# Three products of constants per slot, added to open sums in 14 of 104 slots of each batch but the last

## The chip, the cores and the metric

The kernel runs on one core of a Trainium2 chip. The metric is the device time of that core in microseconds (us); before the change the median of three runs is 1739.21 us (1738.99 to 1742.22). Engines by their short names: PE is TensorE (PEld its weight loads), DVE VectorE, ACT ScalarE, POOL GpSimd, SP SyncE. PEclk is the clock that TensorE was granted, as a share of 2.4 GHz: 1.00 is 2.4 GHz, 0.50 is 1.2 GHz, and a value between them is a mean over a stretch that has both.

## The reference

```
h = concat(x[:, 0:744], x[:, 3:747], x[:, 6:750]) @ W.T + b      # 8 x 744 x 256
q, k, v = heads(layernorm(h));  att = softmax(causal(q k^T / 4)) # 16 heads of 16
h = h + (att v) @ Wp.T + bp
x2 = layernorm(h);  logits = x2 @ wr + br;  top 2 of 4 experts, gates = softmax(top 2)
out = h + sum over the 2 chosen of gate * (y_e - c_e + c_sum),  y_e = gelu(x2 @ w1_e + b1_e) @ w2_e + b2_e
```

Here x is 8 x 750 x 256 in fp32, c_e is the expert's output for a zero input, and c_sum the sum of the four.

## The kernel before

Attention goes batch by batch (8 batches). A batch's 744 positions are 6 tiles of 124, and its 16 heads are 4 groups of 4. For every group the scores are formed twice. First in rows (`mx`, tile mxb, line 1409), from which DVE takes each row's maximum (lines 1040 and 1043, result mxp); the maxima are turned on PE (line 1415), made negative and split on DVE (negp) and sent by SP's queue into qst, the stack of queries. Then in columns (`st`, tile stb, line 1428), from which ACT makes the exponentials (prob, line 857) and POOL masks the diagonal (line 709). Products with the values (`pv`, line 1453) add up in two banks called pvb; the 17th of their output rows per head is the sum of weights. mxb and stb have two buffers each, so PE can be two steps ahead of DVE and of ACT.

The order is written out by hand. `body_events` makes the list of a batch: 104 slots, 26 for each group. Slot s begins with `st` s, then come the `mx` steps due there, then what `put(s, ...)` sets beside it. Every engine runs through the same list and does its own part, in order. So one batch's attention lies beside the previous batch's end (`proj`, the output projection and second norm, line 1389 on PE and 1074 on DVE; `scale2`, `gate`, `count`, `scatter`, the routing to experts) and beside the next batch's front (`tok`, the input layer; `xn`, its norm, DVE line 1013; `turn`, its transposes, PE line 1363; `qk`, its queries and keys, line 1341 with xnT and qkvw, from which ACT, DVE and POOL make `parts` that SP stores to qk_s and loads again as stacks qst and kst).

Points that matter here:

- `turn` 2 and 3 stand in slots 35 and 36 and wait for all six `xn`, the last of which DVE makes in slot 34.
- `st` 26 g waits for the negated maxima of group g (negm_loaded): slots 0, 26, 52 and 78.
- `mx` of the next batch's first group begins in slot 67 and waits for its stack (stack_loaded).
- `pv` of group 0 stands in slots 12, 20, 24, 28, 28 and 30, that of group 1 in 38, 46, 50, 54, 54 and 56. A sum in the second bank is open from a group's first `pv` to its last.
- `earlier` is a 124 x 124 bf16 constant, 1 above the diagonal and 0 elsewhere, so its column 0 is zero; `every` is all ones. Both serve `count` (lines 1397, 1398).

After the eighth batch the experts run: 34 tiles of 384 tokens, `l1` (line 1505) and `l2` (line 1521).

Of the kernel before, what the change touches and what calls it, by code (L numbers as in the profile page):

```python
# [16 lines left out]
TT = T // NT  # L17
HALF = T // 2
NH, DH = 16, 16
# [41 lines left out]
LEAD = 12  # L61
PV_LAG = 4
PB = 3


def part_at(n, t):
# [4 lines left out]
def later(value):  # L71

    return not isinstance(value, int) or value > 0


def mx_events(first, last):

    for u in range(first, last):
        yield "mx", u
        g, k = divmod(u, NMX)  # L80
        if g and k in (1, 3, 4):
            yield {1: "mx_row", 3: "mx_turn", 4: "mx_neg"}[k], g - 1
# [23 lines left out]
def pv_events(g):  # L106

    for o in range(NT):
        yield NST * g + PV_AFTER[o] + PV_LAG, ("pv", (g, o))
    yield NST * (g + 1) + PV_LAG + 1, ("pv_copy", g)  # L110


def body_events(first, last):


    beside = {}

    def put(s, *event):
        beside.setdefault(s, []).append(event)

    for g in range(-1 if not first else 0, NG):
        for s, event in pv_events(g):
            if 0 <= s < NG * NST:
                put(s, *event)
    for i in range(NT):
        put(5 + i, "v", i)
        if not last:
            put(11 + 2 * i, "tok", i)
        if not first:
            put(23 + 2 * i, "proj", i)  # L130
    if not first:
        put(6, "fold", -1)
        put(10, "recip", -1)
        put(11, "spread_out", -1)
        put(14, "spread_in", -1)
        put(1, "scale", -2)
        put(20, "scale", -1)
        put(4, "late_stack", 2)
        put(19, "late_stack", NG - 1)
        put(36, "norm2", 0)  # L140
        for i, s in enumerate((39, 40, 42, 43, 45, 46)):
            put(s, "scale2", i)
        put(42, "h2_store", 0)
        for p, s in enumerate((48, 49, 51, 52)):
            put(s, "gate", p)
        put(54, "count", 0)
        put(55, "place", 0)
        put(56, "place", 1)
        for i, s in enumerate((58, 61, 64, 67, 71, 74, 78, 81, 84, 88, 91, 95)):
            put(57 + 2 * i if last else s, "scatter", i)  # L150
    for g, s in ((0, 45), (1, 60), (2, 86)):
        put(s, "fold", g)
    put(73, "recip", 0)
    put(75, "spread_out", 0)
    put(79, "spread_in", 0)
    for n, (load, split, store) in enumerate(((2, 10, 13), (19, 26, 29), (47, 57, 62), (67, 76, 98))):
        if last:
            load, split, store = ((2, 8, 11), (14, 19, 21), (24, 29, 31), (34, 39, 41))[n]
        put(load, "wload", n)
        put(split, "wsplit", n)  # L160
        put(store, "wstore", n)
    if not first:
        put(7, "res_load", -1)
    if last:
        put(64, "res_load", 0)
    if not last:
        for p in range(2 * KC):
            put(2 + 2 * p, "x", p)
        put(22, "norm", 0)
        for i in range(NT):  # L170
            put(24 + 2 * i, "xn", i)
        for n, s in enumerate((30, 32, 35, 36)):
            put(s, "turn", n)
        for p, s in enumerate((35, 36, 37)):
            put(s, "bias", p)
        put(53, "h1_store", 0)
        for n in range(4):
            put(38 + 3 * n, "qk", n)
            put(59 + 3 * n, "qk", n + 4)
        put(51, "load_stack", 0)  # L180
        put(72, "load_stack", 1)
        put(35, "x_load", 1)
    else:
        for s, kind in ((68, "mx_row"), (70, "mx_turn"), (72, "mx_neg")):
            put(s, kind, NG - 1)
        for m, s in enumerate(W2_SLOT):
            put(s, "w2_load", m)
        put(30, "early_consts", 0)
        put(58, "early_table", 0)
        put(50, "small_load", 0)  # L190
        put(74, "early_load", 0)
        put(86, "early_load", 1)
    mx_at = NMX + LEAD
    mx_end = NG * NMX if last else NG * NMX + NMX + LEAD
    for s in range(NG * NST):
        want = min(NMX + LEAD + (s + 1) * NMX // NST, mx_end)
        g, k = divmod(s, NST)
        yield "st", s
        yield from mx_events(mx_at, want)
        mx_at = max(mx_at, want)  # L200
        for o in range(NT):
            if PV_AFTER[o] == k + 1:
                yield "mask", (g, o)
        yield from beside.get(s, ())
# [124 lines left out]
def layer(nc, xT, tokWT, tokW, tokb, wkT, wqT, wvT, wpT, wp, bp, bcols, wr, br, wall, h1_s, qk_s, r_s, out, ws, xs, b1T, b2, base):  # L329
    with ExitStack() as es:  # L330
        memory = ExitStack()

        def sb(name, shape, dt=fp32):
            return memory.enter_context(nc.sbuf_tensor(name, shape, dt))

        def ps(name, shape):
            return memory.enter_context(nc.psum_tensor(name, shape, fp32))
# [14 lines left out]
        h1 = sb("h1", [TT, NT, DA])  # L352
        parts = sb("parts", [128, PB, NPART, HALF], bf16)
        rest = sb("rest", [128, 2, HALF])
# [39 lines left out]
        earlier = sb("earlier", [TT, TT], bf16)  # L394
        every = sb("every", [TT, TT], bf16)
# [25 lines left out]
        pvb = ps("pvb", [128, 2, 512])  # L421
# [48 lines left out]
        def sem(name):  # L470
            return es.enter_context(nc.semaphore(name))
# [9 lines left out]
        qk_mid, qk_low = sem("qk_mid"), sem("qk_low")  # L481
        parts_stored = [sem(f"parts_stored{i}") for i in range(PB)]
        stack_loaded = [sem(f"stack_loaded{g}") for g in range(NG)]
# [45 lines left out]
        def _(sp):  # L529
# [12 lines left out]
            def emit(events, b, a):  # L542
                for kind, n in events:
                    if kind == "qk":
# [3 lines left out]
                                     .rearrange("t r h c -> (r h) t c"),  # L548
                                     parts[:, (a * 8 + n) % PB, :, :]).then_inc(parts_stored[(a * 8 + n) % PB], 16)
                    if kind in ("load_stack", "late_stack"):  # L550
                        to = a if kind == "load_stack" else b

                        for i in range(PB):
                            sp.wait_ge(parts_stored[i], 16 * ((to * 8 + n // 2 * 4 + 3 - i) // PB + 1))
                        if later(to):
# [40 lines left out]
                    if kind == "w2_load":  # L596

                        sp.wait_ge(v_full, NB * NT)
                        sp.wait_ge(h1_stored, NB * 16)
                        for i in range(PB):  # L600
                            sp.wait_ge(parts_stored[i], 16 * ((NB * 8 - 1 - i) // PB + 1))
# [705 lines left out]
        def _(pe):  # L1307
            pe.wait_ge(raw_loaded, 32)
            for c in range(3 * KC):
                for k in range(KC):  # L1310
                    done = nc.tensor.matmul(pab[:, NE * c:NE * c + NE], tok_raw[:, k, 128 * c:128 * c + 128], wr_sb[:, k, :],
                                            start=(k == 0), stop=(k == KC - 1))
# [3 lines left out]
            for c in range(KC):  # L1316
                for k in range(KC):
                    nc.tensor.matmul(pabs[1][:, 24 + NE * c:24 + NE * c + NE], wp_rows[:, k, 128 * c:128 * c + 128], wr_sb[:, k, :],
                                     start=(k == 0), stop=(k == KC - 1))
            for n in range(3):  # L1320
                for k in range(KC):
                    side = ones[:, :] if n == 2 else bcol[:, k, n:n + 1].broadcast_to([128, TT])
                    done = nc.tensor.matmul(pabs[1][0:TT, 40 + NE * n:40 + NE * n + NE], side, wr_sb[:, k, :],
                                            start=(k == 0), stop=(k == KC - 1))
# [5 lines left out]
            def take_bank(pab, by, value):  # L1330

                k = pabs.index(pab)
                if bank_by[k] is not None:
                    pe.wait_ge(*bank_by[k])
                bank_by[k] = (by, value)
# [8 lines left out]
            def emit(events, b, a):  # L1344
                for kind, n in events:
# [3 lines left out]
                    if kind == "tok":  # L1349
                        if n == 0:  # L1350
                            pe.wait_ge(x_split, a * KC + KC)
                        take_bank(pab, tok_evac, a * NT + n + 1)
                        split_product(pab[0:TT, 0:DA],
                                      [[xp[p][:, c, TT * n + o:TT * n + o + TT] for o in SHIFTS for c in range(KC)] for p in range(2)],
                                      [[tokw[p][:, c, :] for c in range(3 * KC)] for p in range(2)]).then_inc(tok_full, 1)
                    if kind == "turn":
                        c, half = n % 2, n // 2
                        if a == 0 and n == 0:
                            pe.wait_ge(consts, 5)
                        pe.wait_ge(xn_ready, a * NT + 3 * half + 3)  # L1360
                        take_bank(pab, turn_evac, a * 4 + n + 1)
                        for i in range(3):
                            done = nc.tensor.transpose(pab[:, TT * i:TT * i + TT], xn[:, 3 * half + i, 128 * c:128 * c + 128],
                                                       ident[0:TT, 0:TT])
                        done.then_inc(turn_full, 1)
# [18 lines left out]
                    if kind == "proj":  # L1384
# [3 lines left out]
                        for c in range(KC):  # L1388
                            done = nc.tensor.matmul(pab[0:TT, 0:DA], yT[:, c, TT * n:TT * n + TT], projw[:, c, :],
                                                    start=(c == 0), stop=(c == KC - 1))  # L1390
# [8 lines left out]
                    if kind == "mx":  # L1399
                        g, k = divmod(n, NMX)  # L1400
# [15 lines left out]
                    if kind == "st":  # L1416
                        g, k = divmod(n, NST)
# [8 lines left out]
                        for j, h, q0, w in ST[k]:  # L1426
                            out = stb[n % STB][0:TT, at:at + w]
                            done = nc.tensor.matmul(out, kst[g][:, h, TT * j:TT * j + TT], qst[g][:, h, q0:q0 + w],  # L1428
                                                    start=True, stop=True)
                            at += w  # L1430
                        done.then_inc(st_full, 1)
                    if kind == "pv":
# [11 lines left out]
                        for s in range(2):  # L1444
# [3 lines left out]
                            for h in range(HG):  # L1448
                                if j in prob:
                                    p = prob[j][0:TT, h, q0 - TT * j:q1 - TT * j]  # L1450
                                else:
# [3 lines left out]
                                                        stop=(j == (2 if s == 0 else 4)))  # L1455
# [117 lines left out]
```

## Time and profile before

| | before |
|---|---|
| median of 3 runs | 1739.21 us |
| profiled execution | 1728.33 us |
| its span, first to last instruction | 1726.6 us |
| mean granted clock | 0.937 |
| PE busy | 1523.0 us (88%) |
| DVE busy | 1101.6 us (64%) |
| POOL busy | 836.9 us (48%) |
| ACT busy | 707.3 us (41%) |

The shares are means over stages that differ: from 98.5 us to 1054.8 us the eight batches run, from about 1180 us on the experts alone. Slots have no record of their own; where one begins is read from its `st` product (line 1428), since the shapes of these come in a fixed order and all 1024 are in the trace. In batch 1, slot 24 begins on PE at 240.5 us, slot 28 at 245.4, slot 34 at 252.7, slot 36 at 256.2, slot 41 at 262.8, slot 52 at 279.5 and slot 60 at 289.7.

### The profile page before, as it was taken

The page shows a single profiled execution, that of the slowest core. Times are in us where ns is not written, and L with a number is a line of the kernel's source. Part 1 is how long each engine was busy: PE and PEld are TensorE (multiplying, and loading weights), DVE is VectorE, ACT ScalarE, POOL GpSimd, SP SyncE. Part 2 cuts the span into 40 slices and gives each one's busy share as a digit, 9 for nine tenths or more (in the row PEclk, how much of TensorE's full clock was granted, in tenths as well). Part 3 has the DMA queues.
Part 4 walks back from the last instruction along what each step waited for, and adds up shares of the span by engine and source line. Part 5 has one row for each costly group of instructions (what it writes and reads, how often), then busy time and mean ns, then how long its engine had stood idle before and what let it go on. Part 6 is the DMA issues. An engine that isn't in the chain of part 4 may idle for free.

```text
span 1726.6 us, 33232 instructions
## 1 busy us (share of the span) xinstructions
PE 1523.0 (88%) x10648; PEld 1185.3 (69%) x10648; DVE 1101.6 (64%) x3477; ACT 707.3 (41%) x1464; POOL 836.9 (48%) x912
## 2 busy tenths in 40 slices
PE   6598898997988988988978777899999999999997
PEld 5364474564564654744745434889999999999997
DVE  3367777677687787687776650755555555555554
ACT  1135644634545545445445443233333333333332
POOL 5315435635536546447356342165564544444445
PEclk9689998999999998999999877999999999999998
DMA  3623635635536536436436764265645546455451
GB/s 109 149 55 98 153 101 146 150 94 164 143 90 181 129 104 174 122 111 179 116 110 167 216 217 146 76 201 183 210 166 185 197 154 208 170 171 189 165 200 38
DMA packets 166972, 256.24 MB, mean 148 GB/s; under 512 B 30484, under 2 KB 97998, under 8 KB 166800
## 3 DMA queue, kind: packets, MB, share of 16 engines
q1 hardware_dynamic: 108816, 166.66, 33.0%
q10 hardware_dynamic: 34368, 50.33, 9.1%
q0 software_dynamic: 23616, 37.12, 7.6%
q8 instruction: 87, 1.43, 0.3%
q14 instruction: 85, 0.70, 0.1%
HBM read 173.92 MB, written 75.29 MB: 144 GB/s over the span
## 4 chain that ended last, share of the span: by engine, by line
PE 51%; DVE 13%; issue 12%; DMA 10%; SPq 5%; POOL 4%; ACT 3%; ACTq 0%; DVEq 0%; POOLq 0%
PE yb L1521 14%; PE l1b L1505 13%; PE pab L1341 8%; PE pvb L1453 5%; PE mxb L1409 4%; PE stb L1428 4%; DVE unused L1040 4%; DMA qk_s<-parts 3%; DMA qst<-negp 3%; SPq L593 2%; POOL xs L698 2%; DVE mxp L1043 2%; SPq L561 1%; PE rb L1470 1%; ACT hf L943 1%
## 5 line engine op out<-in xcount | busy, mean ns | idle before, releaser
L857 ACT ACTIVATE prob<-stb 124x496 f32<-124x496 f32 (+2 forms) x832 | 398.0, 505 | 407.8 <-PE stb L1428 378.4
L1040 DVE CUSTOM_DVE_ANT_0 unused<-mxb,mask_row 124x372 bf16<-124x372 f32 (+4 forms) x768 | 352.2, 484 | 72.7 <-PE mxb L1409 68.9
L1409 PE MATMUL mxb<-kst,qst 96*124 96x372 bf16 (+4 forms) x1024 | 315.9, 341 | 84.4 <-DVE mxp L1040 52.9
L1428 PE MATMUL stb<-qst,kst 99*124 99x372 bf16 (+4 forms) x1024 | 310.1, 336 | 40.9 <-ACT prob L857 19.1
L1521 PE MATMUL yb<-w2p,hp 128*128 x2448 | 335.3, 282 | 12.1 <-DVE yo L1296 11.7
L1505 PE MATMUL l1b<-x2T,w1s 128*128 128x384 f32 x1632 | 339.9, 344 | 1.2 <-DVE x2T L1250 1.2
L1521 PEld LDWEIGHTS yb<-w2p,hp 128*128 128x128 f32 x2448 | 320.8, 189 | 22.6 <-issue 22.6
L943 ACT ACTIVATE hf<-l1b,b1c 128x384 f32<-128x384 f32 x272 | 158.3, 582 | 350.2 <-PE l1b L1505 307.2
L1505 PEld LDWEIGHTS l1b<-x2T,w1s 128*128 128x128 f32 x1632 | 277.9, 190 | 1.5 <-DVE x2T L1250 1.4
L1409 PEld LDWEIGHTS mxb<-kst,qst 96*124 96x124 bf16 x1024 | 138.7, 144 | 175.0 <-DVE mxp L1040 94.7
L1282 DVE CAST hp<-hf 128x384 fp32r<-128x384 f32 x272 | 105.3, 387 | 236.4 <-ACT hf L943 189.5
L1428 PEld LDWEIGHTS stb<-qst,kst 99*124 99x124 bf16 x1024 | 134.9, 141 | 169.9 <-ACT prob L857 85.3
L709 POOL TENSOR_SCALAR_AFFINE_SELECT prob<-prob 124x496 f32<-124x496 f32 x192 | 118.7, 626 | 270.5 <-ACT prob L857 269.0
L1453 PE MATMUL pvb<-prob,vaug 124*17 124x372 f32 (+2 forms) x2304 | 193.9, 454 | 4.1 <-POOL prob L709 3.9
L698 POOL DMA_INDIRECT xs<-xrow,place x96 | 132.9, 1385 | 109.5 <-issue 109.5
L1284 DVE TENSOR_TENSOR hp<-hf,hp 128x384 fp32r<-128x384 f32 x272 | 163.3, 600 | 9.4
L1043 DVE TENSOR_REDUCE mxp<-mxb 124x1 f32<-124x372 f32 (+1 forms) x256 | 129.8, 507 | 48.6 <-PE mxb L1409 45.3
L770 POOL DMA_INDIRECT acc<-out,xg x102 | 107.3, 1052 | 109.6 <-DMA out<-acc,xg 88.5
L776 POOL TENSOR_TENSOR acc<-acc,yo 128x256 f32<-128x256 f32 x102 | 84.3, 848 | 145.7 <-DVE yo L1296 125.7
L779 POOL DMA_INDIRECT out<-acc,xg x102 | 105.9, 1038 | 26.3 <-issue 20.7
L1341 PE MATMUL pab<-tokw,xp 128*124 128x260 f32 x864 | 117.9, 292 | 0.0
L1341 PEld LDWEIGHTS pab<-tokw,xp 128*124 128x124 f32 x864 | 109.8, 188 | 1.1
(178 smaller groups left out, 1492.9 us busy)
## 6 DMA issues: line engine op xcount, KB each, us to landing
w1s<-ws SPq DMA_DIRECT2D x34, 2048.0 KB
qk_s<-parts SPq DMA_DIRECT2D x64, 279.0 KB
xg<-xs SPq DMA_DIRECT2D x34, 396.0 KB
kst<-qk_s SPq DMA_DIRECT2D x32, 279.0 KB, 3.7
qst<-qk_s SPq DMA_DIRECT2D x32, 279.0 KB, 5.2
wraw<-in_w_all ACTq DMA_DIRECT2D x32, 256.0 KB
ws<-whi ACTq DMA_DIRECT2D x32, 256.0 KB
ws<-wlo ACTq DMA_DIRECT2D x32, 256.0 KB
```

The lines of the kernel that those rows point to most:

```text
L698: pool.indirect_dma_start(out=xs, out_offset=bass.IndirectOffsetOnAxis(ap=place[:, k, i:i + 1].bitcast(u32), axis=0), in_=xrow[:, i, :], i ...
L857: act.activation(dst, src, ACT.Exp, scale=DH ** -0.5).then_inc(exp_done, 1)
L943: act.activation(hf[:, n % HFB, :], l1b[n % L1B][:, 0:TILE], ACT.Gelu, bias=b1c[:, bass.ds(owners[t] * NM + m, 1)]).then_inc(gelu_done, 1)
L1040: done = dve.tensor_tensor_reduce(out=unused[:, n % 2, e * w:(e + 1) * w], in0=src, in1=mask_row[:, T - w:T], scale=1.0, scalar=-3.0e38, o ...
L1043: done = dve.tensor_reduce(top, src, AX.X, ALU.max)
L1284: dve.tensor_tensor(hp[1][:, n % HPB, :], hf[:, n % HFB, :], hp[0][:, n % HPB, :].bitcast(fp32), ALU.subtract).then_inc(h_split, 1)
L1341: done = nc.tensor.matmul(out, lhs[x][c], rhs[w][c], start=(n == 0), stop=(n == len(steps) - 1))
L1409: done = nc.tensor.matmul(out, qst[g % NG][0:ROWS, h + e, TT * i:TT * i + TT], kst[g % NG][0:ROWS, h + e, k0:k0 + w], start=True, stop=True)
L1428: done = nc.tensor.matmul(out, kst[g][:, h, TT * j:TT * j + TT], qst[g][:, h, q0:q0 + w], start=True, stop=True)
L1453: done = nc.tensor.matmul(pvb[2 * DH * h:2 * DH * h + DH + 1, s, q0 - s * HALF:q1 - s * HALF], vaug[:, j, HG * (g % NG) + h, :], p, start= ...
L1505: done = nc.tensor.matmul(l1b[n % L1B][:, 0:TILE], w1s[t % 2][:, w, c, 128 * m:128 * m + 128], x2T[x][:, t % 2, c, :], start=(k == 0), sto ...
L1521: done = nc.tensor.matmul(yb[i][:, 0:D], hp[x][:, n % HPB, 128 * i:128 * i + 128], w2p[w][:, bass.ds(owners[t], 1), m, :], start=(m == 0 a ...
```

## The change

A new event `keep_busy` is set in slots 24 to 27 and 41 to 50 of every batch but the last. PE alone acts on it: three products of 124 columns whose stationary side is column 0 of `earlier`, repeated 17 times, and whose moving side is `every`. Each adds exact zeros to columns 0 to 123 of the first head's rows in the second bank of pvb, with neither start nor stop flag, and with no wait and no semaphore.

```diff
+KEPT_BUSY = tuple(range(24, 28)) + tuple(range(41, 51))
...
         put(store, "wstore", n)
+    if not last:
+        for s in KEPT_BUSY:
+            put(s, "keep_busy", 0)
     if not first:
         put(7, "res_load", -1)
...
+                    if kind == "keep_busy":
+                        for k in range(3):
+                            nc.tensor.matmul(pvb[0:DH + 1, 1, 0:TT], earlier[:, 0:1].broadcast_to([TT, DH + 1]), every[:, :],
+                                             start=False, stop=False)
                     if kind == "turn":
```

The order on PE, batch 1, slots 24 to 27, before (stb opens a slot, mxb are the row scores, pab<-projw the projection, pvb the value sums):

```order
L1428 MATMUL stb<-qst,kst 124x248 x2
L1409 MATMUL mxb<-kst,qst 124x310
L1453 MATMUL pvb<-prob,vaug 17x124 x4
L1453 MATMUL pvb<-prob,vaug 17x372 x4
L1428 MATMUL stb<-qst,kst 124x248 x2
L1409 MATMUL mxb<-kst,qst 124x310 x2
L1389 MATMUL pab<-projw,spare 124x260 x2
L1428 MATMUL stb<-qst,kst 124x372
L1409 MATMUL mxb<-kst,qst 124x310
L1428 MATMUL stb<-qst,kst 124x372
L1409 MATMUL mxb<-kst,qst 124x310
L1389 MATMUL pab<-projw,spare 124x260 x2
```

The same slots with the change (its lines stand 7 or 11 further down):

```order
L1439 MATMUL stb<-qst,kst 124x248 x2
L1420 MATMUL mxb<-kst,qst 124x310
L1464 MATMUL pvb<-prob,vaug 17x124 x4
L1464 MATMUL pvb<-prob,vaug 17x372 x4
L1365 MATMUL pvb<-every,earlier 17x124 x3
L1439 MATMUL stb<-qst,kst 124x248 x2
L1420 MATMUL mxb<-kst,qst 124x310 x2
L1400 MATMUL pab<-projw,spare 124x260 x2
L1365 MATMUL pvb<-every,earlier 17x124 x3
L1439 MATMUL stb<-qst,kst 124x372
L1420 MATMUL mxb<-kst,qst 124x310
L1365 MATMUL pvb<-every,earlier 17x124 x3
```

Nothing changed its place; each slot ends with three products more (slot 27's stand behind its projection, past these rows).

PE again, batch 1, slots 49 to 52, with the change (the third qk product, slot 47, is a few rows above):

```order
L1420 MATMUL mxb<-kst,qst 124x310
L1365 MATMUL pvb<-every,earlier 17x124 x3
L1439 MATMUL stb<-qst,kst 124x248 x2
L1420 MATMUL mxb<-kst,qst 124x310
L1464 MATMUL pvb<-prob,vaug 17x124 x4
L1464 MATMUL pvb<-prob,vaug 17x372 x4
L1365 MATMUL pvb<-every,earlier 17x124 x3
L1439 MATMUL stb<-qst,kst 124x248 x2
L1420 MATMUL mxb<-kst,qst 124x310 x2
L1439 MATMUL stb<-qst,kst 124x372
```

The last three products stand ahead of slot 51's `st`; behind them, in slots 51 and 52, nothing is added. The order on DVE, ACT, POOL and SP is the same as before.

## Rows read from the trace of the kernel before

**Rows 1.** The page: busy time, and the granted clock in 40 slices

```profile
PE 1523.0 (88%) x10648; PEld 1185.3 (69%) x10648; DVE 1101.6 (64%) x3477; ACT 707.3 (41%) x1464; POOL 836.9 (48%) x912
PEclk9689998999999998999999877999999999999998
```

**Rows 2.** Busy time by stretch, columns first: batches 1, 6, 7, experts

```profile
core 0: us, PE busy (x) PEld busy (x) DVE busy (x) ACT busy (x) POOL busy (x), PEclk, DMA share, GB/s
208.50:330.10 121.60, 107.77 (x778) 70.43 (x778) 90.22 (x332) 58.21 (x127) 64.48 (x71) 0.93 0.51 136
...
819.00:941.00 122.00, 106.77 (x779) 69.60 (x779) 91.00 (x335) 58.35 (x128) 64.96 (x71) 0.94 0.48 129
941.00:1054.80 113.80, 89.63 (x570) 44.29 (x573) 58.84 (x237) 53.82 (x115) 44.51 (x54) 0.81 0.71 209
1180.00:1726.60 546.60, 525.33 (x3729) 515.86 (x3727) 304.58 (x650) 201.57 (x384) 274.90 (x283) 0.99 0.51 171
```

**Rows 3.** Busy time by stretch, batch 1: slots 24-28, 28-34, then around the fall

```profile
240.40:245.40 5.00, 4.58 (x38) 2.96 (x35) 4.90 (x18) 2.02 (x4) 4.23 (x6) 1.00 0.89 174
245.40:252.70 7.30, 7.30 (x55) 4.66 (x54) 7.20 (x23) 4.20 (x9) 1.06 (x2) 1.00 0.19 72
253.09:256.51 3.42, 1.26 (x8) 0.79 (x7) 3.12 (x11) 0.81 (x3) 1.22 (x1) 1.00 0.00 0
256.51:259.92 3.41, 3.41 (x19) 1.70 (x20) 2.95 (x16) 1.85 (x5) 1.27 (x1) 0.50 0.69 227
```

**Rows 4.** Timeline, batch 1, slots 34 and 35: start, duration, [idle before]

```profile
254.26 0.37 PE L1409 MATMUL mxb<-kst,qst 96*124 96x372 bf16 x1 [0.95 <-DVE mxp L1040]
255.38 0.41 DVE L1013 TENSOR_SCALAR xn<-h,mv,rstd 124x256 f32<-124x256 f32 x1
255.84 0.54 PE L1363 MATMUL pab<-ident,xn 124*128 124x124 f32 x3 [1.21 <-DVE xn L1013]
```

**Rows 5.** Busy time by stretch, before the slot-35 fall, batches 0 and 6

```profile
140.47:143.88 3.41, 1.82 (x11) 1.24 (x11) 2.73 (x9) 1.08 (x4) 3.41 (x3) 1.00 0.14 18
...
864.05:867.46 3.41, 1.24 (x9) 0.98 (x9) 2.92 (x10) 0.79 (x3) 1.01 (x1) 1.00 0.00 0
```

**Rows 6.** Busy time by stretch, slots 36 to 41, batches 1 and 2

```profile
256.20:262.80 6.60, 6.46 (x42) 3.94 (x40) 3.53 (x20) 2.76 (x8) 3.86 (x3) 0.74 0.36 119
378.40:386.60 8.20, 7.65 (x42) 4.76 (x40) 3.54 (x20) 2.75 (x8) 3.84 (x3) 0.58 0.28 95
```

**Rows 7.** Timeline of PE, batch 1, slots 51 and 52

```profile
276.38 0.34 PE L1409 MATMUL mxb<-kst,qst 96*124 96x310 bf16 x1 [0.45 <-DVE mxp L1043]
278.09 0.34 PE L1409 MATMUL mxb<-kst,qst 96*124 96x310 bf16 x1 [1.37 <-DVE mxp L1040]
279.52 0.37 PE L1428 MATMUL stb<-qst,kst 99*124 99x372 bf16 x1 [1.09 <-DMA qst<-negp]
```

**Rows 8.** Busy time by stretch, slots 52 to 60, batches 2 and 4

```profile
402.90:411.70 8.80, 7.63 (x48) 3.97 (x49) 7.45 (x32) 4.43 (x10) 2.80 (x3) 0.81 0.51 143
647.40:658.20 10.80, 10.64 (x48) 5.79 (x49) 7.32 (x31) 4.56 (x10) 3.88 (x4) 0.50 0.58 165
```

**Rows 9.** Timeline of PE, batch 1, slot 66: four products of 124 columns

```profile
296.49 0.39 PE L1409 MATMUL mxb<-kst,qst 96*124 96x124 bf16 x4
296.71 0.30 PE L1428 MATMUL stb<-qst,kst 99*124 99x310 bf16 x1
```

**Rows 10.** Timeline, batch 1: a projection and its reader, a qk product and its readers

```profile
247.06 1.04 PE L1389 MATMUL pab<-projw,spare 128*124 128x260 f32 x4
248.51 0.42 DVE L1074 TENSOR_TENSOR res<-pab,res 124x260 f32<-124x260 f32 x1
...
271.35 1.31 PE L1341 MATMUL pab<-xnT,qkvw 128*128 128x372 f32 x6
272.69 0.48 ACT L910 ACTIVATE parts<-pab 128x372 bf16<-128x372 f32 x1 [0.59 <-PE pab L1341]
273.20 0.55 DVE L1027 TENSOR_TENSOR rest<-pab,parts 128x372 f32<-128x372 f32 x1 [0.64 <-ACT parts L910]
```

**Rows 11.** Waits of PE, 208.5 to 941.0 us: total, times, longest

```profile
PE stb L1428 <- DMA qst<-negp: 13.0, 13, 3.1
PE mxb L1409 <- DMA qst<-qk_s: 8.1, 4, 3.6
```

## The prediction

> **What bounds the kernel now.** I read the page first. PE is busy 88% of the span, DVE 64%, and TensorE's granted clock has dips all through the batches and nearly none in the experts [rows 1]. By stretch, a batch of the seven that the change touches takes 120 to 126 us at a mean clock of 0.93 to 0.96, the last batch, which gets no new product, has 0.81, and the experts 0.99 [rows 2]. So what the change can give back lies in batches 0 to 6: a mean of 0.93 over 121.6 us is 2 x 0.07 x 121.6 = 17 us at half clock in batch 1, and 122 x 0.06 x 2 = 15 us in batch 6.
>
> Next, where a batch waits. Batch 1 is the pattern, and the others repeat it within some tenths of a us. From slot 24 to 34 PE and DVE are both full: DVE 4.90 of 5.00 and 7.20 of 7.30 us [rows 3]. Then DVE is late. PE stands still 0.95 us for a free mxb buffer and 1.21 us for the last `xn` [rows 4]: 2.2 us in a stretch of 3, PE busy 1.26 of 3.42 us, and in the next 3.41 us the clock is 0.50 [rows 3]. This fall stands behind slot 35 in all seven batches. PE had been busy 1.82 us before the first and 1.24 before the last [rows 5]; in batches 0, 2, 3 and 4 it was 1.7 to 1.8, in 1, 5 and 6 about 1.25.
>
> A second stretch like it stands at slots 51 and 52: 0.45 and 1.37 us for mxb buffers, 1.09 us for the negated maxima of group 2 [rows 7]. The clock falls there in batches 1 to 6. Other falls, at slots 67 to 77 of some batches, stand behind waits for the stacks [rows 11] and have no new product near.
>
> **What the change adds.** 14 slots x 7 batches x 3 = 294 products on PE, and nothing on another engine or queue. The trace has no such product. The nearest row is four bf16 products of 124 columns; they start at 296.49 and the next product at 296.71, so 0.22 us / 4 = 55 ns each at full clock [rows 9]. Three are 0.165 us, all 294 are 16.2 us. If all of it lay on the path, the change would cost 16.2 us and more at half clock; if PE waits anyway, it costs nothing. These are the two ends of the direct cost. The Trainium skill (TensorE: Matmul & The Clock Gate, Back-to-back issue gap) puts a stream of weight load and product pairs at about 81 ns per product of 128 columns; by that the 294 would be an estimated 23.8 us. The trace's 55 ns for just such pairs is lower, and the sum goes by it.
>
> **Slots 24 to 27: what hides them.** 4 x 0.165 = 0.66 us per batch. PE's next wait behind them is the 0.95 us for DVE in slot 34, so it is DVE that has to be late for the same work. What DVE takes from PE in between is there early: the projection of slot 29 starts its last merged row at 247.06, ends at 248.10, and DVE takes it at 248.51, so 0.4 us of room [rows 10]. Of 0.66 us, 0.26 could then show at this one reader, and later readers have more room. Ends: 0 and 0.66 us per batch; I take 0.1, near the row's zero, 0.7 us in seven batches.
>
> **Slots 41 to 50.** 10 x 0.165 = 1.65 us per batch. Up to slot 46 PE mostly waits for DVE, so these are mostly hidden. From 46 on PE leads: DVE stood idle 0.64 us and ACT 0.59 before they could take the qk product of slot 47 [rows 10]. The three or so slots ahead of it delay it by up to 0.5 us, and it leads by way of `parts` and the store to the stack that slot 67 waits for. What is added behind slot 47 only shortens the wait at slots 51 and 52. Ends: 0 and 1.65; I take 0.15 per batch, since four batches at most wait at slot 67 [rows 11], 1.0 us in all. Direct cost 0.7 + 1.0 = 1.7 us.
>
> **What it gives back.** The 0.66 us from slots 24 to 27 move PE's work later, into its waits at slots 34 and 35: the 0.95 us wait shrinks to some 0.3, and before the fall PE is busy 1.8 to 1.9 us instead of 1.25, and about 2.4 instead of 1.8 in batches 0, 2, 3 and 4. I take it that the fall goes in these four and in one of the other three: five of seven. That is the step I am least sure of, since no row shows what would be enough. Price of one fall: slots 36 to 41 hold the same work in every batch and take 6.60 us at a mean clock of 0.74 and 8.20 us at 0.58, twice the half-clock time [rows 6]; one stretch of 3.4 us at half clock costs 1.6 us. DVE waits for PE there (busy 3.53 of 6.60), so it is on the path. 5 x 1.6 = 8.0 us.
>
> At slots 51 and 52 the new products fill the first 0.45 us wait, while the 1.37 us (DVE, in its gate arithmetic) and the 1.09 us (a DMA) remain [rows 7]. I let two of six falls go. Slots 52 to 60 take 8.80 us at 0.81 (2 x 0.19 x 8.80 = 3.3 us at half clock) and 10.80 us at 0.50 (10.8 us) [rows 8]: 2.0 us for 7.5 us, 0.27 us per us. A fall lasts from 3.3 us (batch 2) to past these 10.8 us (batch 4), I take 6.8: 1.8 us each, 3.6 us for two. Half of it is eaten at slot 67, where PE waits for the next stack by up to 3.6 us [rows 11] and would only wait longer: 1.8 us. The Trainium skill (the same page, HAM oscillation) prices clock loss at half the throttled time. By that the two falls give 2 x 6.8 x 0.5 = 6.8 us, an estimate, and the trace's own 0.27 is lower because DVE (7.45 of 8.80 us busy) holds this stretch too. For slots 36 to 41 the rule would give 1.7 us each, and rows give 1.6.
>
> Sum: -8.0 - 1.8 + 1.7 = -8.1 us. The profiled execution took 1728.33 us, its span 1726.6; it would come to about 1720. The median of the runs, 1739.21, stands 10.9 us above the profiled one, which I keep: 1739.2 - 8.1 = 1731 us.
>
> **Rivals.**
> 1. *Both places hold the clock.* All 7 + 6 falls go: 7 x 1.6 = 11.2 and 6 x 1.8 = 10.8, less a third for the waits at slot 67, 7.2; with 1.7 of cost, -16.7 us: 1722.5. For it: at slots 51 and 52 the products behind slot 47 bring up to 0.8 us of work nearer to the wait. Against: 1.37 + 1.09 us of standing still are not touched.
> 2. *Given back at the stacks.* Falls at slot 35 go, but what is won is lost again to the DMA waits at slots 52, 67 and 78, 13.0 + 8.1 us in six batches [rows 11], and stretches of low work there drop the clock anew. For it: these waits follow DMA chains that PE does not speed up, and a long pause has cost the clock wherever one stood. Against: the chains start from `qk` and from the maxima, which come earlier by the same 1.6 us. About 0: 1739.
> 3. *The clock falls all the same and the products cost.* Slower. The place is slots 24 to 29 and 44 to 47: PE late by 0.66 us at the projection that had 0.4 us of room, and by 0.5 us at the third qk product with none. 0.26 + 0.5 = 0.8 us per batch, 5.3 us in seven: 1744.5. It decides if fewer than three falls go (3 x 1.6 = 4.8). For it: before the falls of batches 1, 5 and 6 PE was busy only 1.25 us. Against: DVE is 98% busy in slots 24 to 34 and PE's delay is mostly in its shadow.
> 4. *The products do nothing*, because so narrow a product, of zeros, may not hold a clock. Then only the moved work counts, which the forecast already rests on; it would come to somewhere between the forecast and rival 3.
>
> **How the numbers follow.** The forecast has 0.42 (its own range 1725 to 1735), rival 1 0.16, rival 2 0.20, rival 3 with what of 4 goes to it 0.22. Moving the work by tenths of a us also shifts where later pauses lie against the clock's falls, the untouched last batch at 0.81 among them, and I allow 3 us either way for it. A measurement of this kernel can tell about 0.2%, 3.5 us, from no change. Faster by more than that: the forecast and rival 1, with a little of 2: 0.60. Within it 0.21, slower 0.19. The range goes from 1719, below rival 1, to 1744, at rival 3.
>
> **What would show it.** In the profile after: slots 36 to 41 at clock 1.00 in about five of the batches 0 to 6, and 5.0 to 5.4 us long where they were 6.6; the wait for mxb before slot 35 down from 0.95 to about 0.3, while that for `xn` stays; the wait of 0.45 us in slot 51 gone; the new products at some 55 ns apart. Batches 0 to 6 at a mean clock of 0.96 to 0.97, batch 7 as before. It is wrong if the slot-35 falls remain in five batches or more, if DVE in slots 28 to 34 shows waits for the projection that were not there, or if the time between slots 60 and 78 grows by what the earlier slots gave.

## The result and the profile after

The kernel became slower: 1750.66 us median of 20 runs against 1737.76 of 20 runs of the kernel before beside them, ratio 1.0074 (95% interval 1.0055 to 1.0093), about 13 us. Repeated in two other sessions the ratio was 1.0082 (1.0049 to 1.0116) and 1.0094 (1.0058 to 1.0129). Forecast were 8 us less.

The page of the profiled execution, lines as in [rows 1]:

```profile
span 1747.4 us, 33820 instructions
PE 1551.6 (89%) x10942; PEld 1203.4 (69%) x10942; DVE 1107.6 (63%) x3477; ACT 709.8 (41%) x1464; POOL 835.2 (48%) x912
PEclk9689998998898999999989887999999999999998
```

The span is 20.8 us longer than in the one execution before, PE is busy 28.6 us more, and the dips of the clock lie nearly where they were. By stretch, batch 1 with the change (slots 24 to 28, 28 to 34, before and behind the fall, then slots 36 to 41 and 52 to 60; the columns are those of [rows 2]):

```profile
245.20:251.40 6.20, 5.78 (x49) 3.46 (x48) 6.11 (x17) 2.13 (x4) 4.98 (x6) 1.00 0.74 140
251.40:258.60 7.20, 7.20 (x56) 4.70 (x55) 6.35 (x21) 4.21 (x9) 0.20 (x1) 1.00 0.20 73
260.10:263.50 3.40, 1.82 (x11) 1.24 (x11) 2.68 (x11) 0.62 (x2) 0.21 (x1) 0.99 0.05 8
263.50:266.90 3.40, 3.05 (x19) 1.03 (x19) 2.61 (x16) 1.33 (x4) 2.25 (x2) 0.50 0.61 218
262.30:270.60 8.30, 7.75 (x42) 4.82 (x40) 3.67 (x19) 2.87 (x8) 3.85 (x3) 0.59 0.27 93
287.40:297.20 9.80, 9.16 (x49) 4.51 (x50) 7.55 (x34) 4.54 (x10) 2.68 (x3) 0.65 0.54 148
```

Slots 24 to 28 take 6.20 us where they took 5.00 by [rows 3] (6.2 and 4.9 in every batch from 1 to 6). In slots 28 to 34, PE is full as before, but DVE, busy 7.20 of 7.30 us before, is now busy 6.35 of 7.20: it waits for PE, once for a projection, the sign of being wrong that the prediction named. In the same stretch before, DVE has no such wait. Its waits from 251.4 to 258.6 us:

```profile
DVE res L1081 <- PE pab L1400: 0.4, 1, 0.4
DVE unused L1047 <- PE mxb L1420: 0.3, 1, 0.3
```

And the clock falls behind slot 35 all the same, in seven of seven batches here; in the two further profiles of the change (after_again, after_third) it was seven and six. The waits of [rows 4] were to shrink; they are here:

```profile
260.27 0.37 PE L1420 MATMUL mxb<-kst,qst 96*124 96x372 bf16 x1 [1.12 <-DVE mxp L1047]
261.39 0.41 DVE L1020 TENSOR_SCALAR xn<-h,mv,rstd 124x256 f32<-124x256 f32 x1
261.85 0.54 PE L1374 MATMUL pab<-ident,xn 124*128 124x124 f32 x3 [1.21 <-DVE xn L1020]
```

1.12 and 1.21 us instead of 0.95 and 1.21, the same in each of batches 1 to 6. DVE moved by as much as PE did, so PE stands still as long as ever, only later. What one block of three products costs, from the timeline of PE, slots 24 and 26 of batch 1:

```profile
246.20 1.03 PE L1464 MATMUL pvb<-prob,vaug 124*17 124x124 f32 x16
247.05 0.33 PE L1365 MATMUL pvb<-every,earlier 124*17 124x124 bf16 x3
247.31 0.42 PE L1439 MATMUL stb<-qst,kst 99*124 99x248 bf16 x2
...
249.28 0.30 PE L1420 MATMUL mxb<-kst,qst 96*124 96x310 bf16 x1
249.50 0.33 PE L1365 MATMUL pvb<-every,earlier 124*17 124x124 bf16 x3
249.76 0.37 PE L1439 MATMUL stb<-qst,kst 99*124 99x372 bf16 x1
```

and slot 26 before:

```profile
244.07 0.29 PE L1409 MATMUL mxb<-kst,qst 96*124 96x310 bf16 x1
244.20 0.32 PE L1428 MATMUL stb<-qst,kst 99*124 99x372 bf16 x1
```

From the score product to the next slot's `st` it was 0.13 us and is 0.48: the block costs 0.35 us, not 0.165. Behind a value product (slot 24; there `st` began 0.97 us after the `pv` block's start and now begins 1.11 after) it costs 0.14. As means over batches 1 to 6, slots 24 to 27 grew by 0.14, 0.35, 0.40 and 0.40 us, 1.30 together. The second place, slots 50 to 52 of batch 1, answers to [rows 7]:

```profile
284.96 0.34 PE L1420 MATMUL mxb<-kst,qst 96*124 96x310 bf16 x1 [0.31 <-DVE mxp L1050]
286.82 0.34 PE L1420 MATMUL mxb<-kst,qst 96*124 96x310 bf16 x1 [1.51 <-DVE mxp L1047]
287.34 0.57 PE L1439 MATMUL stb<-qst,kst 99*124 99x372 bf16 x1 [0.18 <-DMA qst<-negp]
```

2.0 us of waiting where there were 2.9 (the 0.45 us became 0.31 and did not go), and the clock fell there too.

Since single stretches scatter, this table holds means over batches 1 to 6 of one profiled execution of each kernel: us between the `st` products of two slots, and in brackets us at half clock (2 x (1 - granted clock) x length; not given where it was 0.5 or less in every column).

| slots | before | after | mx_wide | fill_35_wide | fill_both | fill_both_fold |
|---|---|---|---|---|---|---|
| 24-28 | 4.91 | 6.21 | 5.59 | 4.91 | 4.91 | 4.91 |
| 28-34 | 7.35 | 7.22 | 7.17 | 7.35 | 7.34 | 7.34 |
| 34-36 | 3.50 | 3.76 | 3.72 | 3.49 | 3.50 | 3.50 |
| 36-41 | 7.09 (4.0) | 7.05 (3.8) | 7.26 (4.4) | 5.68 (0) | 5.68 (0) | 5.68 (0) |
| 41-47 | 8.21 | 8.74 | 8.55 | 7.92 | 7.91 | 7.91 |
| 47-51 | 4.45 | 5.04 | 4.78 | 4.50 | 4.62 | 4.63 |
| 51-52 | 3.65 | 2.90 | 2.98 | 3.99 | 3.97 | 4.04 |
| 52-60 | 9.66 (6.6) | 10.25 (8.0) | 10.47 (8.5) | 9.05 (5.2) | 7.49 (0) | 7.60 (0) |
| 60-67 | 6.91 | 6.89 | 6.89 | 7.22 | 7.08 | 7.18 |
| 67-78 | 13.99 (1.8) | 14.48 (2.4) | 13.47 (0.9) | 16.06 (3.5) | 19.22 (7.2) | 15.63 (3.0) |

### The profile page after: what moved, and what is told of

Same layout as the page of the kernel before. It is cut to its first block, busy times and chain, and to the rows that moved or that the text cites. A ratio compares the mean times of both kernels' runs of the same rounds, so it can differ in the third digit from the quotient of the medians.

```text
span 1747.4 us, 33820 instructions
## 1 busy us (share of the span) xinstructions
PE 1551.6 (89%) x10942; PEld 1203.4 (69%) x10942; DVE 1107.6 (63%) x3477; ACT 709.8 (41%) x1464; POOL 835.2 (48%) x912
## 3 DMA queue, kind: packets, MB, share of 16 engines
q8 instruction: 89, 1.46, 0.4%
## 4 chain that ended last, share of the span: by engine, by line
PE 57%; DVE 11%; issue 10%; DMA 10%; SPq 5%; POOL 4%; ACT 3%; ACTq 0%; DVEq 0%; POOLq 0%
PE yb L1532 14%; PE l1b L1516 13%; PE pab L1348 8%; PE pvb L1464 6%; PE stb L1439 5%; PE mxb L1420 5%; DMA qk_s<-parts 3%; DVE unused L1047 3%; DMA qst<-negp 3%; SPq L600 2%; DMA qst<-qk_s 2%; PE pab L1400 1%; POOL xs L705 1%; PE rb L1481 1%; ACT hf L950 1%
## 5 line engine op out<-in xcount | busy, mean ns | idle before, releaser
L1464 PEld LDWEIGHTS pvb<-prob,vaug 124*17 124x17 f32 x2304 | 53.6, 102 | 83.3 <-issue 64.1
```

Source lines behind the costliest of these rows:

```text
L1464: done = nc.tensor.matmul(pvb[2 * DH * h:2 * DH * h + DH + 1, s, q0 - s * HALF:q1 - s * HALF], vaug[:, j, HG * (g % NG) + h, :], p, start= ...
```

## Experiments

Theory A, after the result: the loss is direct. PE paces slots 24 to 34, each block costs twice the forecast, and the clock is not held because the products do not stand where PE stands still. Rivals: the loss is made in slots 41 to 50 alone; narrow products of zeros do not hold a clock; moving the work against the clock's falls did it. The last has no experiment of its own. Slots 24 to 28 took 6.21 us in each of batches 1 to 6, so their cost does not hang on it; for slots 52 to 60 it stays open.

**The two parts.**

```diff
-KEPT_BUSY = tuple(range(24, 28)) + tuple(range(41, 51))
+KEPT_BUSY = tuple(range(24, 28))      # only_24_27
+KEPT_BUSY = tuple(range(41, 51))      # only_41_50
```

> The products stand in slots 24 to 27 alone. Theory A (the whole delay of these slots goes through to the end, because from slot 24 to 34 PE is the pacer and DVE follows it): slots 24 to 28 take 6.2 us instead of 4.9, slots 34 to 37 keep their 2.2 us of standing still, and 7 x 1.3 = 9 us are lost, ratio about 1.005. Rival B (the loss is made in slots 41 to 50, and DVE hides slots 24 to 27 as predicted): within 2 us of before, ratio 1.000 to 1.001, with the waits at slots 34 and 35 shorter by some 0.7 us.

> The products stand in slots 41 to 50 alone. Theory A: slots 41 to 47 take 0.6 us longer in each of seven batches, what is added behind slot 47 only shortens the waits at slots 51 and 52 by about 0.8 us; 7 x 0.6 = 4 us lost, ratio 1.002 to 1.003. Rival B: all of the loss, 13 us, ratio 1.007. Rival C (moving work into the waits holds the clock at slot 52): slots 52 to 60 shorter by 1.8 us in two batches or more, ratio below 1.001.

Measured 1.0023 (0.9996 to 1.0049) and 1.0001 (0.9978 to 1.0024): too little by far for the whole. In the profiles slots 24 to 28 took 6.21 us and slots 34 to 36 3.69 in the first, slots 41 to 47 8.74 and 47 to 51 5.05 in the second, just as with the whole change, so the local costs stood as theory A had them and only the sum did not. Both parts and the whole were then run in one session:

> Slots 24 to 27 alone, repeated beside the whole change in one session. Alone they measured 1.0023 [0.9996, 1.0049], slots 41 to 50 alone 1.0001 [0.9978, 1.0024], both 1.0074 and 1.0082. Theory J (slot 67 hides the first microsecond or two of any delay, since PE then waits less for the next stack; both parts together use this cover up): the parts stay at 1.002 to 1.003 and 1.000 to 1.001, their sum well under the whole. Rival K (they add up, and a session's scatter hid it): this one 1.004 to 1.006.

> Slots 41 to 50 alone, repeated likewise. Theory J: 1.000 to 1.001. Rival K: 1.002 to 1.004.

> The whole change beside its two parts. Theory J and rival K both: 1.006 to 1.009; it is the sum that the two parts are to be held against.

Measured 1.0048 (1.0029 to 1.0067), 1.0033 (1.0011 to 1.0055) and 1.0094 (1.0058 to 1.0129). The parts add up to 1.0081, which speaks for rival K against theory J of a shared cover. It does not settle it: with both sessions weighted by their intervals the parts come to 1.0039 and 1.0018, 1.0057 together, against 1.0079 for the three measurements of the whole, and the difference, 0.0022, is within the noise of 0.0027. The repeat ahead of it:

> The changed kernel itself once more, beside the fillers of this call. Slots 24 to 27 alone measured 1.0023, slots 41 to 50 alone 1.0001, and both together 1.0074 in another session. Theory A (the parts add up, and the first session or the parts are off by their scatter): 1.003 to 1.006. Rival (the parts hurt each other, by later pauses that grow only when both are there): 1.007 to 1.009 again.

1.0082 (1.0049 to 1.0116), between the other two measurements of the whole.

**Width and number.** mx_narrow and mx_wide write the same number of products in the same slots to the score bank, just ahead of the product that overwrites it; they differ only in WIDE, which is 17 (DH + 1) or 124 (TT). Against the kernel before:

```diff
+        if not last and s in KEPT_BUSY:
+            yield "keep_busy", 0
         yield from mx_events(mx_at, want)
...
+                    if kind == "keep_busy":
+                        padding.append(3)
...
+                        for k in range(padding.pop() if padding else 0):
+                            nc.tensor.matmul(mxb[n % MXB][0:WIDE, 0:TT], earlier[:, 0:1].broadcast_to([TT, WIDE]), every[:, :],
+                                             start=True, stop=True)
```

> The same number of products in the same slots, but written to the score bank mxb right before the slot's score product overwrites it, 17 output rows wide as in the change. Theory A (a block of products 17 wide among products 124 wide costs some 0.1 us at each change of width, beside 55 ns for each product): a slot grows by about 0.35 us where PE does not wait, and the kernel is about 13 us slower, ratio 1.006 to 1.008. Rival B (a product simply costs 0.11 us here): the same. The place differs from the change: behind the wait for DVE, not ahead of it, so up to 0.2 us per waiting slot could be less hidden, ratio up to 1.012.

> As mx_narrow, but each product 124 output rows wide, the width of its neighbours. Theory A (the change of width is half of the cost): the first of the three starts without a gap behind its neighbour, a slot grows by 0.165 us where PE does not wait, the sum of the change's cost is halved, and the kernel is 4 to 7 us slower than before, ratio 1.002 to 1.004, clearly faster than mx_narrow. Rival B (three products cost 0.33 us whatever their width): same time as mx_narrow. Rival C (wide products hold the clock, narrow ones do not): half-clock stretches behind slot 35 or 52 go in three batches or more, ratio under 1.000.

The timeline of PE in slot 26, narrow, then wide:

```profile
248.96 0.32 PE L1441 MATMUL stb<-qst,kst 99*124 99x372 bf16 x1
249.21 0.33 PE L1418 MATMUL mxb<-every,earlier 124*17 124x124 bf16 x3
249.47 0.34 PE L1422 MATMUL mxb<-kst,qst 96*124 96x310 bf16 x1
249.65 0.32 PE L1441 MATMUL stb<-qst,kst 99*124 99x372 bf16 x1
```

```profile
246.81 0.32 PE L1441 MATMUL stb<-qst,kst 99*124 99x372 bf16 x1
246.97 0.33 PE L1418 MATMUL mxb<-every,earlier 124*124 124x124 bf16 x3
247.14 0.30 PE L1422 MATMUL mxb<-kst,qst 96*124 96x310 bf16 x1
247.27 0.32 PE L1441 MATMUL stb<-qst,kst 99*124 99x372 bf16 x1
```

`st` to `st` is 0.69 us narrow and 0.46 wide; without products it is 0.29 (243.91 to 244.20 in the trace of before). So 0.17 us for three wide ones, 55 ns each as forecast, and 0.40 for three narrow ones: the change of width costs some 0.2 us a block. That much is shown. The total does not show it: 1.0058 (1.0036 to 1.0081) and 1.0050 (1.0028 to 1.0072) can't be told apart, where theory A had half the loss for the wide ones. Slots 24 to 28 lost 0.68 instead of 1.46 us, but slots 52 to 60 were 0.8 us longer than before in mx_wide too.

One product per slot instead of three (`range(1)` for `range(3)`):

> The change with one product per slot instead of three. Theory A (a block has a fixed price for the change of width, about 0.2 us, beside 0.055 us per product): slots 24 to 28 take 4 x 0.25 = 1.0 us longer than before where three per slot take 1.3, and slots 47 to 51 0.45 us; the kernel is 8 to 11 us slower, ratio 1.004 to 1.006. Rival (the price goes with the number, 0.11 us each): 0.45 us in slots 24 to 28, 4 us in all, ratio 1.002.

1.0083 (1.0061 to 1.0105). Slots 24 to 28 took 5.77 us, 0.86 more than before against 1.30 with three: most of a block's price does not go with its number, as theory A says. The two further products in each of the four blocks cost 0.44 us, 55 ns each. That the total was no smaller at all was not expected; slots 52 to 60 were 10.52 us long, with 8.1 us at half clock. In all eight profiles with products in slots 41 to 50 that figure is 7.2 to 9.5 us, in those without them 6.6 or less.

**Products where PE stands still.** None of the change's products; instead `fill` events in the waits.

fill_both is shown. fill_35_wide has no products in slots 50 and 51 (counts and MID are 0); fill_35_narrow too, with WIDE = DH + 1 and 8 and 14 products.

```diff
+KEPT_BUSY = ()
+WIDE = TT
+FILL = ((34, 10), (35, 16), (50, 3), (51, 14))
+MID = 16
...
+        for s, count in FILL:
+            if count:
+                put(s, "fill", (s, count))
...
+        if s == 51 and MID and not last:
+            steps.insert(1, ("fill", (51, MID)))
...
+                    if kind == "fill":
+                        s, count = n
+                        if s < 38:
+                            pe.wait_ge(pv_copied, b * NG + 1)
+                        for k in range(count):
+                            if s < 38:
+                                nc.tensor.matmul(pvb[0:WIDE, 1, 0:TT], earlier[:, 0:1].broadcast_to([TT, WIDE]), every[:, :],
+                                                 start=True, stop=True)
+                            else:
+                                nc.tensor.matmul(pvb[0:DH + 1, 1, 0:TT], earlier[:, 0:1].broadcast_to([TT, DH + 1]), every[:, :],
+                                                 start=False, stop=False)
```

The 16 of MID stand between slot 51's two score products.

> No products of the change. Instead zeros are multiplied while PE waits for DVE: 10 products at the end of slot 34 and 16 in slot 35 ahead of turn 2, 124 rows wide, 0.55 and 0.88 us, into the value bank between two groups. Theory D (what counts is PE's standing still before the fall; the change missed it, since its products lie 7 slots ahead and the wait only moves with them): the half-clock stretch behind slot 35 goes in five or more of seven batches, slots 36 to 41 take 5.0 to 5.4 us instead of 7.1, and the kernel is 8 to 11 us faster, ratio 0.994 to 0.996. Rival E (zeros do not hold the clock, or the fall follows from something earlier): falls as before, and the ratio is 1.000 to 1.003.

> The same place with products 17 rows wide, 8 and 14 of them. Theory D: as fill_35_wide. Rival F (a narrow product does not count for the clock as a wide one does): falls stay in four batches or more while fill_35_wide loses them; ratio 0.999 to 1.002.

> fill_35_wide, and narrow products of zeros in the second long wait too: 3 at the end of slot 50, 16 between the two score products of slot 51, 14 at its end. Theory D: the half-clock stretch behind slot 52 goes too in four or more of six batches, slots 52 to 60 take 7 to 8 us instead of 9.7, and half of that is lost again at slot 67; 5 us more than fill_35_wide, ratio 0.990 to 0.994. Rival F: only slot 35 changes.

Measured 0.998 (0.9953 to 1.0007), 0.9969 (0.9943 to 0.9994) and 1.0009 (0.9986 to 1.0032). By stretch, slots 34 to 36 and 36 to 41 of batch 1 in fill_35_wide:

```profile
259.49:262.99 3.50, 2.81 (x35) 2.35 (x34) 3.47 (x12) 0.86 (x2) 1.59 (x2) 1.00 0.00 0
262.99:268.66 5.67, 4.94 (x42) 3.23 (x41) 3.54 (x20) 2.78 (x8) 3.25 (x3) 1.00 0.44 135
```

The stretch that was 3.50 us long still is: 26 products fitted into its waits for nothing. The clock holds, and slots 36 to 41 take 5.67 us instead of 6.60 [rows 6], the same in all of batches 1 to 6 and in fill_35_narrow; no fall is left behind slot 35 in seven batches. That is theory D for the clock, and rivals E and F fall: zeros, in products 17 rows wide, hold the clock. For the time it had 8 to 11 us; the medians gave 3.5 and 5.4 us, the wide one's interval has 1 in it, and here too PE waited longer for the stack, 18.9 us in batches 1 to 6 of fill_35_wide against 8.1 [rows 11]. In fill_both the second fall goes too, in all six batches (slots 52 to 60 of batch 1), and then PE waits for the next stack:

```profile
283.17:290.63 7.46, 6.24 (x48) 3.54 (x49) 5.88 (x29) 4.20 (x10) 2.59 (x3) 1.00 0.38 106
297.96:305.91 7.95, 0.66 (x5) 0.37 (x4) 1.37 (x9) 0.96 (x3) 4.24 (x5) 0.79 0.85 236
```

Slot 67, the last of these stretches, has PE busy 0.66 of 7.95 us. The waits of PE over the batches, second line of [rows 11], in fill_both:

```profile
PE mxb L1440 <- DMA qst<-qk_s: 38.0, 6, 7.8
```

8.1 us had become 38.0: the 3.2 us per batch won between slots 34 and 67 were lost there, and some more. So rival 2 of the prediction is real, once there is a gain to give back. Theory D's time for fill_both, a ratio of 0.990 to 0.994, was missed by this.

**Why slot 67 waits.** The stack's loads follow the store of the fourth qk part. SP's queue in the trace of before, batch 1:

```profile
273.97 1.42 SPq L547 DMA_DIRECT2D qk_s<-parts  x1
275.51 1.29 SPq L574 DMA_DIRECT2D sums<-spare  x1
276.85 2.45 SPq L577 DMA_DIRECT2D spare<-spare  x4
279.34 1.37 SPq L547 DMA_DIRECT2D qk_s<-parts  x1
```

Five transfers of group 0's finished value sums (`fold`, slot 45) stand between the third store and the fourth. fold_48 moves them behind the fourth.

```diff
-    for g, s in ((0, 45), (1, 60), (2, 86)):
+    for g, s in ((0, 48), (1, 60), (2, 86)):
```

> The kernel before with the fold of group 0 moved from slot 45 to 48, nothing else. In the trace of before, the fourth qk part is ready at 275.3 us and stored at 279.3, because SP issues the fold's five transfers in between. Theory G (slot 67 waits for a chain of DMAs that starts with this store): the store starts 3 to 4 us earlier, the waits at slot 67 (8.1 us in six batches, and the short ones behind) go, and the kernel is 2 to 8 us faster, ratio 0.995 to 0.999. Rival H (the stores and loads are bound by the traffic of the DMA queues and land when they did): 1.000.

> fill_both with the fold moved likewise. fill_both holds the clock at both places, is at slot 67 about 3.5 us earlier in its batch than before, and then waits there 3 to 8 us. Theory G: that wait shrinks by 3 to 4 us in each of six batches, the gain of the held clock reaches the end, and the kernel is 15 to 25 us faster than fill_both, ratio 0.985 to 0.993. Rival H: as fill_both, 1.000 to 1.002.

0.9965 (0.9943 to 0.9988) for the fold alone, and 0.992 (0.9896 to 0.9945) with fill_both, some 14 us faster than before. SP's queue in fold_48, batch 1:

```profile
281.62 2.81 SPq L547 DMA_DIRECT2D qk_s<-parts  x2
284.56 0.60 SPq L574 DMA_DIRECT2D sums<-spare  x1
285.20 5.11 SPq L577 DMA_DIRECT2D spare<-spare  x4
290.47 4.61 SPq L561 DMA_DIRECT2D kst<-qk_s  x3
```

The two stores are issued together. Against slot 34 of its batch, the fourth store came 4.0 us earlier than before in the mean of batches 1 to 6, and the first load of the stack 2.6 us earlier. In fold_48's own profile PE still waited 5.3 us for the stack where it was 8.1, so that profile accounts for half of its 6 us. And the waits of PE in fill_both_fold:

```profile
PE mxb L1440 <- DMA qst<-qk_s: 16.9, 6, 5.4
```

21 us less waiting than in fill_both, and theory G holds in its direction; of the 3 to 4 us per batch it had, 3.5 came.

Two more fillers, 40 or 20 narrow products in slot 67 ahead of the score product that waits:

```diff
+        if s == 67 and not last:
+            steps.insert([e[0] == "mx" and e[1] == NG * NMX for e in steps].index(True), ("fill", (67, 40)))
```

> fill_both and 40 more narrow products of zeros (2.2 us) in slot 67, ahead of the score product that waits for the next stack. If the wait there is 3 to 8 us, they fit in it, and the half-clock stretch behind slot 67 (7 us per batch between slots 67 and 78) goes in most batches where the wait is below 5 us: 0.25 us for each us of half clock, some 5 to 8 us in all against fill_both, ratio 0.996 to 0.998. If the products are not enough for so long a wait, the falls stay and the ratio is that of fill_both, 1.001.

> fill_both_fold with 20 narrow products of zeros more (1.1 us) in slot 67 ahead of the score product that waits for the next stack; its waits there were 1.5 to 5.4 us. If they keep the clock in the four batches whose wait is below 3 us, 3 to 6 us faster than fill_both_fold: ratio 0.989 to 0.991. If PE loses its lead where the wait has gone, 0.992 to 0.995.

1.0019 (1.0002 to 1.0037) and 0.9925 (0.9899 to 0.9951): nothing beyond fill_both and fill_both_fold. In fill_three three of the falls behind slot 67 went and four stayed, but the time there is a DMA's: PE's waits for the stack came to 24.8 us in batches 1 to 6, less than the 38.0 of fill_both by just the 2.2 us of products in each of the six. So PE was held up at slot 67 as long as in fill_both, part of it by products of zeros. fill_both_fold and fill_three_fold are the best versions; they can't be told apart.

## Why the prediction was wrong

The forecast was -8.1 us, the sum of 9.8 us given back and 1.7 us of direct cost. Measured were 13 us more: no fall was given back, and the losses were many times 1.7.

- *Where the clock falls and what one fall costs* was right: slots 36 to 41 at full clock take 5.7 us instead of 7.1 in the mean, 1.4 us per fall where the prediction had 1.6, and it is on the path.
- *Slots 24 to 27: what hides them* is the step that failed first. It held DVE's 98% for a sign that DVE is late and PE has room, and took 0.1 us per batch of a 0 to 0.66 range. Slots 24 to 28 grew by 1.30 us and DVE waited for PE in slots 28 to 34. Both engines were full there, PE to 4.58 of 5.00 and 7.30 of 7.30 [rows 3], and DVE had 0.4 us of room at one projection [rows 10]. The 1.30 us put into four slots had become 1.43 by slot 36. The prediction had these rows and still charged 0.1.
- *The price of a product*, 55 ns, was right for products as wide as their neighbours. The nearest row was 124 wide, the new product 17, and the change of width costs 0.2 us a block: 0.35 to 0.40 instead of 0.165. So the upper end of the direct cost, 16.2 us, was no upper end: 98 blocks at 0.35 to 0.40 are 34 to 39 us. The trace of before had rows of that kind, the value products, before which the weight loads sat idle without a wait that the profile shows. The waits of PEld for these before, and for the new products after:

```profile
PEld pvb L1453 <- issue: 64.0, 246, 0.6
PEld pvb L1365 <- issue: 24.9, 111, 0.3
```

Each is 0.26 or 0.22 us long. That they are the price of the change of width is likely, not shown.

- *What it gives back*, the largest term (8.0 and 1.8 us), failed with the second step: products ahead of a wait were to move work into it. Since DVE moved as well, the wait stayed (0.95 and 1.21 us became 1.12 and 1.21) and all seven falls behind slot 35 stayed. PE's busy time in the 3.4 us before each fall, by which the prediction measured the gain, did not rise as forecast (1.8 to 1.9 us, or 2.4): in batches 1 to 6 it was 1.82, 1.09, 1.08, 1.76, 1.82 and 1.91 us after and 1.25, 1.70, 1.76, 1.81, 1.25 and 1.27 before. It moved both ways while the waits were the same in all six. The fillers show the idea was right and the place wrong: the same products inside the wait cost nothing and hold the clock in every batch.
- *Slots 41 to 50* lost 0.53 us up to slot 47 and 0.59 up to 51, got 0.75 back in the wait as forecast, and then 0.59 were lost behind slot 52, where the half clock lasted 8.0 us instead of 6.6. That it got longer was nowhere in the sum; I took 0.15 us per batch, and alone these slots cost 1.0001 and 1.0033 in two sessions. Why the stretch is longer stays open: the pause ahead of it was shorter, 2.0 instead of 2.9 us in batch 1.
- *Rival 3* named the side, its condition (fewer than three falls go) and its place, at 1744.5 us. With the measured growth of its two places it is 1.3 + 0.5 us per batch, 12.6 us. That this meets the measured 13 is partly luck, as it leaves out what was lost from slot 47 to 60.
- *A misreading beside the point:* not all seven batches take 120 to 126 us. Batch 0 takes 110.0 us before (98.50 to 208.50).

The sum of the measured stretches, 1.4 us for slots 24 to 36 and 0.9 for 36 to 60, makes 2.35 us per batch. With batch 0, where slots 24 to 60 grew by 3.45 us, that is 17.5 us if all of it lay on the path; the three measurements of the time showed 13 to 16. It rests on one profile of the kernel before, whose time, 1728.33 us, was 9.4 us below the median. Slots 67 to 78 are not in it: 13.99 us before, and 14.48, 13.84 and 14.17 in three profiles of the change.

## What to carry to other kernels

To hold TensorE's clock here, filler products had to stand inside the pause that precedes the fall, behind the last thing another engine waits for; a few slots ahead they only delayed everybody, and the pause with them. Inside a wait their width did not matter; outside one, narrow products among wide ones cost twice as much. Before that, look which wait comes next: a gain on PE of 3 us per batch was worth nothing until a DMA chain of another stage had been shortened, which was worth 0.35% by itself and, with the fillers, 0.8%. An engine that was 98% busy beside another that was 100% busy hid nothing of what was added to the other.

## What the runs showed of the hardware

- A block of three products with 17 output rows among products with 124 costs PE 0.35 to 0.40 us (0.14 behind value products, which have 17 rows themselves), the same three with 124 rows 0.17. One product with 17 rows costs 0.25 to 0.29 us there (`one`, slots 25 to 27).
- Products of exact zeros, 17 rows wide, kept the clock at 2.4 GHz as well as wide ones did: no fall behind slot 35 in seven batches with either, and with narrow ones none from slot 51 to 67 in any batch of the four profiles that have them there.
- Half clock went with 0.16 to 0.38 us of device time per us: the runs of the kernel before, time against half-clock time of each run, have a slope of 0.27 (35 runs), 0.38 (30), 0.22 (23) and 0.16 (26) in four sessions. A slope shows no cause. In slots 36 to 41, with the work the same and the clock held, it was 1.4 us for 4.0 us, 0.35 per us.
- In fill_both PE got to slot 67 about 3.2 us sooner in its batch and waited 5 us more for the stack. Its fourth store was issued 0.8 us earlier than before, but its first load 0.9 us later (means over batches 1 to 6, against slot 34): 6.5 us from store to load instead of 4.8. The DMA share in batch 1's wait was 0.85. What the transfers compete with there was not tried.
